# Three stacked graph attention layers: the steps behind a chunk's sums stand earlier and closer together in a table of step numbers

## The chip, the core and the metric

The kernel runs on one core of a Trainium2 chip. A core has five engines with an instruction stream each: TensorE (PE in the profile), VectorE (DVE), ScalarE (ACT), GpSimd (POOL) and SyncE (SP), which here only starts DMAs. An engine takes its instructions strictly in the order in which they are written, and waits at semaphores for the others. The metric is the device time of one execution in microseconds (us), less is better.

## The reference

Three graph attention layers on 3125 nodes, 128 features wide, over the same 103125 edges plus a loop at each node; layers 1 and 2 have a 256-wide hidden part between them, and layers 2 and 3 a layer norm. Each layer is, cut to what matters:

```python
h = x @ W
e = leaky_relu(s[src] + d[dst], 0.2)          # s = h @ a_src, d = h @ a_dst
ex = exp(e - segment_max(e, dst)[dst])
z = segment_sum(ex, dst)
out = segment_sum((ex / z[dst])[:, None] * h[src], dst) + b
```

and the whole: `h = relu(layernorm(x))`, layer 1, `relu`, layer 2, `x = x + ...`, `h = relu(layernorm(x))`, layer 3, `x = x + ...`.

## The kernel before

**Counts instead of edges.** The kernel first (up to about 243 us) turns the edge list into a matrix of counts `C`, 125 partitions wide: how many edges go from each source node to each target. Then every layer is dense: for each target a sum over all sources of count times weight times feature row. Nodes come in 25 tiles of 125.

**Chunks and steps.** The targets are cut into 5 chunks of 5 tiles (625 columns). Three layers of 5 chunks are 15 chunks, `q` = 0 to 14, chunk `q` of layer `q // 5`. A chunk has 25 steps `s`, one for each tile of sources. In a step a block of 125 x 625 weights (`slot[s]`) is made, and PE multiplies it with the feature rows `hB3[:, s]` and adds five sums in PSUM (`products`, L1552; the last two steps L1560). A block is made in one of two ways: by DVE in one instruction (`product`, L924), or by ACT in three (`row_maximum`, L1318, L1321, L1323) and POOL in one (`block_product`, L581). Layer 2 gives the odd steps to ACT and POOL, layer 3 the even ones. ACT works six steps ahead (`PASS_AHEAD`): at its own step s it prepares the block of step s + 6. DVE also computes, for the next chunk's maximum per target, 25 tops (`top_step`, L846 and L848), most of them one to each step.

**What follows a chunk's sums.** Once chunk q - 1 is summed, its result is finished inside the steps of chunk q, by small instructions woven into the streams:

- PE transposes the tops at step `tops` (`top_transpose`, L1522).
- DVE, the chain: `mu` (L858, reads the transposed tops), `e_top` (L861), `m_top` (L864), `back` (L871). Each reads the one before.
- ACT: `kappa` = exp(`back`) (`factors`, L1300). In the stream it stands before the passes of its step.
- DVE, the inverse of the sums: `zk` (L888, needs `kappa`), a reciprocal (L896; in layer 3 L892 and L894), `rz` (L901).
- POOL: `scaled` (L586, needs `rz`) and the addition to `x` (L595). Layer 2: DVE `bn_stats` (L908) and `bn_aggr` (L914), POOL `norm_scalars`, ACT `normalise` (L1264), PE `feat_transposes` (L1575), ACT `copy_featT` (L1235), PE `new_features` (L1608), ACT `new_features` (L1256, L1257).

A table of step numbers sets where each stands. `At(tops, chain, kappa, z, stats, pool, pe, act, rest_pe, rest_act)` has a tuple of steps for each kind of work, and `post_at(q)` picks the row: `USUAL` for most chunks, `BEFORE_LAST` for the last chunk of layers 1 and 2, and `TURN` for a chunk that begins a layer (the turn). A step number is only a place in the streams; nothing but the order depends on it. Chunks 6, 7 and 8 finish chunks of layer 2 by `USUAL[1]`, chunk 9 by `BEFORE_LAST[1]`, chunk 10 by `TURN[1]`, chunks 11 to 14 finish chunks of layer 3 by `USUAL[2]`. Chunk 9 also computes the extremes for layer 3 (L775, L799 at step 6 after an exchange by DMA, and POOL's `scalars` at step 11), and the turn the rest of them (`extremes_late`, L775 again, at step 19), which reads what ACT's `new_features` wrote.

There is a second, slow path (`careful`) for inputs outside a range; these inputs don't take it. It used the table `USUAL` too.

## Time and profile before

| | |
|---|---|
| time, median of 3 runs | 778.18 us (778.1 to 778.4) |
| the profiled execution | 777.95 us, its span 775.9 us, so 2.05 us lie outside the span |
| DVE busy | 713.2 us, 92% of the span |
| PE busy | 664.9 us, 86% |
| ACT busy | 532.1 us, 69% |
| POOL busy | 343.0 us, 44% |
| mean granted TensorE clock | 0.946 |

The span runs from the first to the last instruction that the profiler recorded. Busy time is what an engine spent inside instructions, waits excluded where they come ahead of the instruction. An instruction on DVE is recorded with its own duration, but the next may start before it ends, so the cost of one in a full stream is read from one start to the next.

### The profile page before, as it was taken

The page shows a single profiled execution, that of the slowest core. Times are in us where ns is not written, and L with a number is a line of the kernel's source. Part 1 is how long each engine was busy: PE and PEld are TensorE (multiplying, and loading weights), DVE is VectorE, ACT ScalarE, POOL GpSimd, SP SyncE. Part 2 cuts the span into 40 slices and gives each one's busy share as a digit, 9 for nine tenths or more (in the row PEclk, how much of TensorE's full clock was granted, in tenths as well). Part 3 has the DMA queues.
Part 4 walks back from the last instruction along what each step waited for, and adds up shares of the span by engine and source line. Part 5 has one row for each costly group of instructions (what it writes and reads, how often), then busy time and mean ns, then how long its engine had stood idle before and what let it go on. Part 6 is the DMA issues. An engine that isn't in the chain of part 4 may idle for free.

```text
span 775.9 us, 14060 instructions
## 1 busy us (share of the span) xinstructions
PE 664.9 (86%) x5692; PEld 645.5 (83%) x5692; DVE 713.2 (92%) x935; ACT 532.1 (69%) x814; POOL 343.0 (44%) x305
## 2 busy tenths in 40 slices
PE   4345999898886999999999989999988988998994
PEld 4335888888885989999999989898878888898894
DVE  5499999999976999999999899999999989999994
ACT  0054344444446988778777798898977897898981
POOL 1504000000004555445375556475677666675762
PEclk9997789898876999999999999999999999999997
DMA  3400000000002000000011010000011010100001
GB/s 97 118 0 1 1 1 2 1 1 1 1 1 16 9 17 18 1 17 2 1 8 34 1 25 8 10 17 1 1 8 34 1 25 1 33 23 13 18 1 38
DMA packets 22062, 11.77 MB, mean 15 GB/s; under 512 B 12253, under 2 KB 19915, under 8 KB 21990
## 3 DMA queue, kind: packets, MB, share of 16 engines
q1 hardware_dynamic: 21190, 9.53, 5.5%
q0 software_dynamic: 800, 1.26, 0.6%
q8 instruction: 47, 0.77, 0.5%
q14 instruction: 25, 0.20, 0.1%
HBM read 9.14 MB, written 1.64 MB: 14 GB/s over the span
## 4 chain that ended last, share of the span: by engine, by line
DVE 35%; PE 18%; issue 11%; DMA 2%; POOL 1%; ACT 1%; DVEq 0%; SPq 0%; POOLq 0%
DVE ps L846 18%; PE ps L1552 14%; DVE scratch L924 8%; DVE ps L848 3%; PE ps L1605 1%; DVE mu L858 1%; DMA ext_lines<-ext 1%; PE ps L1583 1%; DMA gathered<-ext_lines 1%; DVE bn6c L908 1%; DVE scratch L846 1%; DVE e_top L861 1%; DVE m_top L864 1%; PE ps L1575 0%; DVE scratch L852 0%
## 5 line engine op out<-in xcount | busy, mean ns | idle before, releaser
L1552 PE MATMUL ps<-hB,scratch 125*125 125x129 f32 x3450 | 408.3, 276 | 34.9 <-DVE scratch L924 27.0
L1552 PEld LDWEIGHTS ps<-hB,scratch 125*125 125x125 f32 x3450 | 392.0, 189 | 47.0 <-DVE scratch L924 38.2
L581 POOL TENSOR_TENSOR scratch<-scratch 125x625 f32<-125x625 f32 x177 | 247.1, 1401 | 181.6 <-ACT scratch L1323 181.4
L846 DVE SCALAR_TENSOR_TENSOR ps<-C,a_unit,ps 125x625 f32<-125x625 uint8 x330 | 279.8, 866 | 2.1
L924 DVE SCALAR_TENSOR_TENSOR scratch<-ps,r_src,C 125x625 f32<-125x625 f32 x198 | 170.7, 862 | 5.4 <-PE ps L1536 5.0
L1487 PE MATMUL ps<-scratch 128*128 128x125 bf16 x1250 | 148.6, 296 | 25.3 <-DVE scratch L760 19.1
L1487 PEld LDWEIGHTS ps<-scratch 128*128 128x128 bf16 x1250 | 143.0, 121 | 29.9 <-DVE scratch L760 23.4
L1323 ACT ACTIVATE scratch<-scratch,r_src 125x625 f32<-125x625 f32 x177 | 158.7, 897 | 0.0
L1318 ACT ACTIVATE scratch<-gathered,r_inv 125x625 f32<-125x625 f32 x177 | 142.9, 807 | 12.8 <-PE ps L1552 10.5
L1198 ACT ACTIVATE C<-ps 125x1750 uint8<-125x1750 f32 (+3 forms) x50 | 74.2, 1488 | 96.9 <-PE ps L1487 96.9
L1321 ACT ACTIVATE scratch<-C 125x625 f32<-125x625 uint8 x177 | 126.3, 714 | 11.1 <-POOL scratch L581 10.8
L760 DVE TENSOR_TENSOR scratch<-key_lo,hB 128x6656 bf16<-128x6656 bf16 (+3 forms) x26 | 94.7, 3642 | 4.5 <-PE ps L1487 4.5
L760 DVE TENSOR_TENSOR scratch<-key_col,hB 128x6500 bf16<-128x6500 bf16 (+3 forms) x26 | 86.0, 3307 | 0.0
L546 POOL TENSOR_TENSOR spread<-extg 125x1 f32<-125x1 f32 x3 | 1.8, 585 | 172.0 <-DVE extg L799 172.0
L1560 PE MATMUL ps<-hB,scratch 125*125 125x129 f32 x300 | 35.5, 273 | 0.0
L1560 PEld LDWEIGHTS ps<-hB,scratch 125*125 125x125 f32 x300 | 34.2, 187 | 0.0
L848 DVE TENSOR_SCALAR ps<-C,a_unit 125x625 f32<-125x625 uint8 x30 | 25.9, 864 | 2.7 <-ACT C L1198 2.6
L1167 ACT ACTIVATE w1T<-ps 128x256 f32<-128x256 f32 x1 | 0.4, 383 | 34.8 <-PE ps L1457 34.8
L1300 ACT ACTIVATE kappa<-back 125x5 f32<-125x5 f32 x15 | 3.1, 208 | 29.4 <-DVE back L871 29.4
L1447 PE MATMUL ps<-ones_b,scratch 125*125 125x1 bf16 x125 | 13.5, 245 | 10.6 <-DVE scratch L705 10.6
L1447 PEld LDWEIGHTS ps<-ones_b,scratch 125*125 125x125 bf16 x125 | 13.4, 230 | 10.6 <-issue 10.6
L586 POOL TENSOR_TENSOR scratch<-scratch,rz 125x640 f32<-125x640 f32 x14 | 17.6, 1258 | 5.9 <-DVE rz L901 5.9
(145 smaller groups left out, 429.9 us busy)
## 6 DMA issues: line engine op xcount, KB each, us to landing
gathered<-g_lines SPq DMA_DIRECT2D x14, 305.2 KB
xr<-in_x SPq DMA_DIRECT2D x1, 1562.5 KB
out<-xr SPq DMA_DIRECT2D x5, 312.5 KB
edge_sb<-in_edges SPq DMA_DIRECT2D x1, 805.7 KB
gathered<-ext_lines SPq DMA_DIRECT2D x5, 122.1 KB
w<-in_W SPq DMA_DIRECT2D x2, 128.0 KB
gathered<-in_edges,start_i POOLq DMA_INDIRECT x5
ext_lines<-ext SPq DMA_DIRECT2D x5, 1.0 KB
```

Of the source, the lines that this page charges most:

```text
L581: g.tensor_tensor(A, A, wide[n % 2], ALU.mult).then_inc(pool_done, 1)
L760: last = v.tensor_tensor(hot[:, g0:g1, :, :], keys.unsqueeze(2).broadcast_to([128, g1 - g0, m, LANES]), iota_t[:, 0:m, :].unsqueeze(1).bro ...
L846: v.scalar_tensor_tensor(dest, counts, unit[:, s:s + 1], top, ALU.min, ALU.max).then_inc(S.top_done, 1)
L848: v.tensor_scalar(dest, counts, unit[:, s:s + 1], None, ALU.min).then_inc(S.top_done, 1)
L924: v.scalar_tensor_tensor(slot[s].rearrange("p (t n) -> p t n", n=P), tiles(ROWU), r_src[L % 2][:, s:s + 1], C5[:, c, s, :].rearrange("p (t ...
L1198: a_.activation(C5[:, c, :, rows].rearrange("p t (w q) -> p t w q", q=WQ), tiles(at_, w1_ - w0).rearrange("p w (t q) -> p t w q", q=WQ), A ...
L1318: a_.activation(A, ga[q % 2], ACT.Relu, bias=-1.0, scale=r_inv[L % 2][:, s:s + 1]).then_inc(over_done, 1)
L1321: a_.activation(wide[k % 2], C5[:, c, s, :], ACT.Copy)
L1323: a_.activation(A, A, ACT.Identity, bias=r_src[L % 2][:, s:s + 1], scale=r_src[L % 2][:, s:s + 1]).then_inc(rowmax_ok, 1)
L1487: last = mm(ps[0:128, o:o + WC], hot_lo[i][:, at_g, :, lane], hot_col[i][:, at_g, :, lane], start=(k == 0), stop=(k == KC - 1))
L1552: last = mm(ps[0:P, acc_at(t):acc_at(t) + HW], A[:, P * t:P * (t + 1)], feat, start=opens and t in (0, 3), stop=closes, skip_group_check=True)
L1560: last = mm(ps[0:P, acc_at(t):acc_at(t) + HW], slot[s][:, P * t:P * (t + 1)], hB3[:, s, :], start=False, stop=s == T - 1, skip_group_check ...
```

## The change

Four rows of the table get other numbers: `USUAL[1]`, `USUAL[2]`, `BEFORE_LAST[1]`, and three numbers in `TURN[1]`. The old `USUAL` is kept under the name `CAREFUL` for the slow path, which so stays as it was. No instruction is added or removed; the first layer's rows are the same. In the diff, with its repeated parts of the slow path cut:

```diff
+        CAREFUL = (At(1, (3, 4, 5, 6), 6, (8, 9, 10), None, (14,), (12, 15, 21), (14, 17, 23), 18, 20),
+                   At(1, (3, 4, 5, 6), 6, (8, 9, 10), (13, 14), (14, 19), (18, None, 21), (16, 20, 23), None, None),
...
         USUAL = (At(1, (3, 4, 5, 6), 6, (8, 9, 10), None, (14,), (12, 15, 21), (14, 17, 23), 18, 20),
-                 At(1, (3, 4, 5, 6), 6, (8, 9, 10), (13, 14), (14, 19), (18, None, 21), (16, 20, 23), None, None),
-                 At(1, (3, 4, 5, 6), 6, (8, 9, 10), None, (14, 17, 20), (None,) * 3, (None,) * 3, None, None))
+                 At(1, (2, 2, 3, 3), 4, (4, 4, 4), (9, 9), (11, 15), (13, None, 15), (13, 14, 17), None, None),
+                 At(1, (2, 2, 3, 3), 4, (4, 4, 4), None, (11, 13, 17), (None,) * 3, (None,) * 3, None, None))
         BEFORE_LAST = (At(1, (3, 4, 5, 6), 6, (8, 9, 10), None, (14,), (12, 14, 19), (13, 16, 21), 17, 18),
-                       At(1, (3, 4, 5, 6), 6, (8, 9, 10), (13, 14), (14, 19), (17, None, 19), (16, 19, 21), None, None))
+                       At(1, (2, 2, 3, 3), 4, (4, 4, 4), (9, 9), (11, 15), (13, None, 15), (13, 14, 17), None, None))
         TURN = (At(None, (1, 1, 2, 2), 3, (3, 3, 3), None, (11,), (7, 9, 13), (9, 12, 15), 11, 13),
-                At(None, (1, 1, 2, 2), 3, (3, 3, 3), (8, 8), (11, 15), (14, None, 16), (13, 14, 17), None, None))
+                At(None, (1, 1, 2, 2), 3, (3, 3, 3), (8, 8), (11, 15), (13, None, 15), (13, 14, 16), None, None))
...
-                at_ = USUAL[q // NC]
+                at_ = CAREFUL[q // NC]
```

DVE in chunk 8 (layer 2), from step 3 to step 6, before. L924 is a block, L846 a top, the rest are the small steps; a row's bracket names the semaphores that it waits for:

```order
L846 SCALAR_TENSOR_TENSOR ps<-C,a_unit,ps 125x625 [waits top_done] x2
L858 TENSOR_REDUCE mu<-ps 125x5 [waits top_T]
L924 SCALAR_TENSOR_TENSOR scratch<-ps,r_src,C 125x625 [waits rows_ready,pe_done]
L846 SCALAR_TENSOR_TENSOR ps<-C,a_unit,ps 125x625 [waits top_done]
L861 SCALAR_TENSOR_TENSOR e_top<-mu,b_low 125x5 [waits top_max,back_low]
L846 SCALAR_TENSOR_TENSOR ps<-C,a_unit,ps 125x625 [waits top_done]
L864 SCALAR_TENSOR_TENSOR m_top<-e_top 125x5 [waits m_lin]
L924 SCALAR_TENSOR_TENSOR scratch<-ps,r_src,C 125x625 [waits rows_ready,pe_done]
L846 SCALAR_TENSOR_TENSOR ps<-C,a_unit,ps 125x625 [waits top_done]
L871 SCALAR_TENSOR_TENSOR back<-m_top,back_of 125x5 [waits kappa_ready,m_lin]
```

The same place in the changed kernel, steps 2 to 4, whose lines are numbered 3 higher:

```order
L849 SCALAR_TENSOR_TENSOR ps<-C,a_unit,ps 125x625 [waits top_done]
L861 TENSOR_REDUCE mu<-ps 125x5 [waits top_T]
L864 SCALAR_TENSOR_TENSOR e_top<-mu,b_low 125x5 [waits top_max,back_low]
L849 SCALAR_TENSOR_TENSOR ps<-C,a_unit,ps 125x625 [waits top_done]
L867 SCALAR_TENSOR_TENSOR m_top<-e_top 125x5 [waits m_lin]
L874 SCALAR_TENSOR_TENSOR back<-m_top,back_of 125x5 [waits kappa_ready,m_lin]
L927 SCALAR_TENSOR_TENSOR scratch<-ps,r_src,C 125x625 [waits rows_ready,pe_done]
L849 SCALAR_TENSOR_TENSOR ps<-C,a_unit,ps 125x625 [waits top_done]
L891 TENSOR_TENSOR zk<-scratch,kappa 125x5 [waits raw_ready,kappa_ready]
L899 RECIPROCAL zk<-zk 125x5 [waits z_lin]
L904 TENSOR_TENSOR rz<-zk,kappa 125x5 [waits raw_used,z_lin]
```

Before, every small instruction had a block or a top between itself and the one that it reads; now four pairs (five with `bn_stats` and `bn_aggr`) are direct neighbours, and `mu` comes one top earlier.

DVE in chunk 12 (layer 3) in the changed kernel, steps 1 to 4:

```order
L927 SCALAR_TENSOR_TENSOR scratch<-ps,r_src,C 125x625 [waits rows_ready,pe_done]
L849 SCALAR_TENSOR_TENSOR ps<-C,a_unit,ps 125x625 [waits top_done] x2
L861 TENSOR_REDUCE mu<-ps 125x5 [waits top_T]
L864 SCALAR_TENSOR_TENSOR e_top<-mu,b_low 125x5 [waits top_max,back_low]
L927 SCALAR_TENSOR_TENSOR scratch<-ps,r_src,C 125x625 [waits rows_ready,pe_done]
```

Before, the second L927 here and one more top stood ahead of `mu`: it comes two instructions earlier.

PE in the turn of layer 3 (chunk 10), where L1575 and L1608 are the transposes and the new features, before and then in the changed kernel:

```order
L1552 MATMUL ps<-hB,scratch 125x129 x75
L1575 MATMUL ps<-ident,scratch 128x125 x5
L1552 MATMUL ps<-hB,scratch 125x129 x10
L1608 MATMUL ps<-w,scratch 125x130 x5
L1552 MATMUL ps<-hB,scratch 125x129 x30
```

```order
L1555 MATMUL ps<-hB,scratch 125x129 x70
L1578 MATMUL ps<-ident,scratch 128x125 x5
L1555 MATMUL ps<-hB,scratch 125x129 x10
L1611 MATMUL ps<-w,scratch 125x130 x5
L1555 MATMUL ps<-hB,scratch 125x129 x35
```

Both moved one step (five matmuls) ahead.

## Rows read from the trace of the kernel before

**Rows 1.** The page, busy time and share of the span of each engine.
```profile
PE 664.9 (86%) x5692; PEld 645.5 (83%) x5692; DVE 713.2 (92%) x935; ACT 532.1 (69%) x814; POOL 343.0 (44%) x305
```

**Rows 2.** Busy time by stretch: chunk 8; order PE, PEld, DVE, ACT, POOL, clock, DMA.
```profile
525.50:559.00 33.50, 31.32 (x275) 30.55 (x275) 33.32 (x57) 29.93 (x50) 21.15 (x18) 1.00 0.01 1
```

**Rows 3.** Timeline, DVE in chunk 8: start, duration, what (x2: two of them).
```profile
528.65 1.64 DVE L846 SCALAR_TENSOR_TENSOR ps<-C,a_unit,ps 125x625 f32<-125x625 uint8 x2
...
544.54 0.84 DVE L846 SCALAR_TENSOR_TENSOR ps<-C,a_unit,ps 125x625 f32<-125x625 uint8 x1
```

**Rows 4.** Timeline, DVE in chunk 10, the turn, steps 1 to 9.
```profile
598.52 0.80 DVE L858 TENSOR_REDUCE mu<-ps 125x5 f32<-125x625 f32 x1
599.44 0.17 DVE L861 SCALAR_TENSOR_TENSOR e_top<-mu,b_low 125x5 f32<-125x5 f32 x1
599.54 0.87 DVE L924 SCALAR_TENSOR_TENSOR scratch<-ps,r_src,C 125x625 f32<-125x625 f32 x1
...
601.10 0.16 DVE L864 SCALAR_TENSOR_TENSOR m_top<-e_top 125x5 f32<-125x5 f32 x1
...
601.38 0.87 DVE L846 SCALAR_TENSOR_TENSOR ps<-C,a_unit,ps 125x625 f32<-125x625 uint8 x1
602.15 0.16 DVE L888 TENSOR_TENSOR zk<-scratch,kappa 125x5 f32<-125x5 f32 x1
...
602.73 0.87 DVE L924 SCALAR_TENSOR_TENSOR scratch<-ps,r_src,C 125x625 f32<-125x625 f32 x1
...
608.23 1.06 DVE L908 BATCH_NORM_STATS2 bn6c<-xr 125x6 f32<-125x128 f32 x5
...
609.68 0.84 DVE L846 SCALAR_TENSOR_TENSOR ps<-C,a_unit,ps 125x625 f32<-125x625 uint8 x1
```

**Rows 5.** Timeline, PE and DVE behind the last chunk; brackets: idle before, releaser.
```profile
764.78 0.71 PE L1522 MATMUL ps<-ident,scratch 125*125 125x125 f32 x5
765.52 0.81 DVE L858 TENSOR_REDUCE mu<-ps 125x5 f32<-125x625 f32 x1 [3.33 <-PE ps L1522]
...
767.28 0.17 DVE L888 TENSOR_TENSOR zk<-scratch,kappa 125x5 f32<-125x5 f32 x1 [0.27 <-ACT kappa L1300]
...
767.91 0.17 DVE L901 TENSOR_TENSOR rz<-zk,kappa 125x5 f32<-125x5 f32 x1
```

**Rows 6.** Timeline, PE and POOL at the head of chunk 8.
```profile
528.77 0.71 PE L1522 MATMUL ps<-ident,scratch 125*125 125x125 f32 x5
...
531.28 1.52 POOL L581 TENSOR_TENSOR scratch<-scratch 125x625 f32<-125x625 f32 x1 [1.70 <-ACT scratch L1323]
```

**Rows 7.** Timeline, heads of chunk 12 and, the last row, of chunk 13.
```profile
672.01 0.71 PE L1522 MATMUL ps<-ident,scratch 125*125 125x125 f32 x5
672.21 0.87 DVE L924 SCALAR_TENSOR_TENSOR scratch<-ps,r_src,C 125x625 f32<-125x625 f32 x1
...
676.16 1.29 POOL L581 TENSOR_TENSOR scratch<-scratch 125x625 f32<-125x625 f32 x1 [1.19 <-ACT scratch L1323]
676.88 0.60 DVE L864 SCALAR_TENSOR_TENSOR m_top<-e_top 125x5 f32<-125x5 f32 x1
...
683.04 0.86 DVE L924 SCALAR_TENSOR_TENSOR scratch<-ps,r_src,C 125x625 f32<-125x625 f32 x1
...
705.12 1.51 POOL L581 TENSOR_TENSOR scratch<-scratch 125x625 f32<-125x625 f32 x1 [0.61 <-ACT scratch L1323]
```

**Rows 8.** Timeline, PE and DVE in the turn, chunk 10, steps 14 to 19.
```profile
617.74 2.37 PE L1552 MATMUL ps<-hB,scratch 125*125 125x129 f32 x20
...
622.18 0.17 DVE L775 TENSOR_SCALAR a_neg<-ab 125x10 f32<-125x10 f32 x1 [3.14 <-ACT ab L1257]
```

**Rows 9.** Timeline, DVE in chunk 9.
```profile
573.62 1.07 DVE L901 TENSOR_TENSOR rz<-zk,kappa 125x5 f32<-125x5 f32 x1
...
578.79 1.07 DVE L908 BATCH_NORM_STATS2 bn6c<-xr 125x6 f32<-125x128 f32 x5 [0.91 <-POOL xr L595]
```

**Rows 10.** Timeline, DVE in chunk 11.
```profile
641.97 1.31 DVE L861 SCALAR_TENSOR_TENSOR e_top<-mu,b_low 125x5 f32<-125x5 f32 x1
```

More of the change, by code:

```diff
@@ L346, in gat_stack_kernel @@
         At = namedtuple("At", "tops chain kappa z stats pool pe act rest_pe rest_act")
+        CAREFUL = (At(1, (3, 4, 5, 6), 6, (8, 9, 10), None, (14,), (12, 15, 21), (14, 17, 23), 18, 20),
+                   At(1, (3, 4, 5, 6), 6, (8, 9, 10), (13, 14), (14, 19), (18, None, 21), (16, 20, 23), None, None),
+                   At(1, (3, 4, 5, 6), 6, (8, 9, 10), None, (14, 17, 20), (None,) * 3, (None,) * 3, None, None))
         USUAL = (At(1, (3, 4, 5, 6), 6, (8, 9, 10), None, (14,), (12, 15, 21), (14, 17, 23), 18, 20),
-                 At(1, (3, 4, 5, 6), 6, (8, 9, 10), (13, 14), (14, 19), (18, None, 21), (16, 20, 23), None, None),
-                 At(1, (3, 4, 5, 6), 6, (8, 9, 10), None, (14, 17, 20), (None,) * 3, (None,) * 3, None, None))
+                 At(1, (2, 2, 3, 3), 4, (4, 4, 4), (9, 9), (11, 15), (13, None, 15), (13, 14, 17), None, None),
+                 At(1, (2, 2, 3, 3), 4, (4, 4, 4), None, (11, 13, 17), (None,) * 3, (None,) * 3, None, None))
         BEFORE_LAST = (At(1, (3, 4, 5, 6), 6, (8, 9, 10), None, (14,), (12, 14, 19), (13, 16, 21), 17, 18),
-                       At(1, (3, 4, 5, 6), 6, (8, 9, 10), (13, 14), (14, 19), (17, None, 19), (16, 19, 21), None, None))
+                       At(1, (2, 2, 3, 3), 4, (4, 4, 4), (9, 9), (11, 15), (13, None, 15), (13, 14, 17), None, None))
         TURN = (At(None, (1, 1, 2, 2), 3, (3, 3, 3), None, (11,), (7, 9, 13), (9, 12, 15), 11, 13),
-                At(None, (1, 1, 2, 2), 3, (3, 3, 3), (8, 8), (11, 15), (14, None, 16), (13, 14, 17), None, None))
+                At(None, (1, 1, 2, 2), 3, (3, 3, 3), (8, 8), (11, 15), (13, None, 15), (13, 14, 16), None, None))
         EXPS = {(0, 0): 1, (1, 0): 2, (1, EARLY_TILES): 3, (1, LATE): 4, (2, 0): 5, (2, EARLY_TILES): 6, (2, LATE): 7}
@@ L1408, in careful_chunk @@
                             careful_sums(q - 1)
-                        after_sums(K, q - 1, USUAL[L], s)
+                        after_sums(K, q - 1, CAREFUL[L], s)
                     if s == LEAD - 1:
@@ L1431, in careful @@
                     for s in range(T):
-                        after_sums(K, L * NC + NC - 1, USUAL[L], s)
+                        after_sums(K, L * NC + NC - 1, CAREFUL[L], s)
             act.wait_ge(mode_ready, 1)
@@ L1716, in careful_chunk @@
                     if c:
-                        after_sums(K, q - 1, USUAL[L], s)
+                        after_sums(K, q - 1, CAREFUL[L], s)
             def careful():
@@ L1727, in careful @@
                     for s in range(T):
-                        after_sums(K, L * NC + NC - 1, USUAL[L], s)
+                        after_sums(K, L * NC + NC - 1, CAREFUL[L], s)
             pe.wait_ge(mode_ready, 1)
```

## The prediction

> **What bounds the kernel now.** I read the page first: DVE is the busiest engine, 713.2 us of the span [rows 1]. Then the busy time by stretch, one stretch to a chunk: in chunk 8 DVE is busy 33.32 of 33.50 us, PE 31.32, ACT 29.93, POOL 21.15 [rows 2], and the other inner chunks of layers 2 and 3 look alike. DVE's stream there has no holes; a chunk lasts as long as DVE's instructions do, laid one behind the other. So a move of steps can gain only where DVE stands still or is held up inside an instruction, and everything that it adds to DVE's stream is paid. That PE, ACT or POOL get a result sooner is worth nothing unless DVE waits for it.
>
> Then the timeline of DVE for its costs from one start to the next. A block or a top costs 0.775 us wherever it stands: from the first top of the pair at 528.65 to the top at 544.54 lie 15.89 us [rows 3] with 17 of them (11 tops, 6 blocks), 13.17 us, so the small steps of a whole chunk of layer 2 cost only 2.72 us: `mu` about 0.72, `bn_stats` and `bn_aggr` 1.32, and the other six 0.07 to 0.11 each, for they overlap with the large neighbour, plus 0.24 held up. In layer 3, chunk 12, from 672.21 to 683.04 are 10.83 us [rows 7] with 11 large ones, 8.53: 2.30 for the small ones.
>
> Last, the holds. Some small DVE instructions last far longer than their 0.15: `m_top` at 676.88 lasts 0.60 and ends at 677.48, and POOL's instruction from 676.16 ends at 677.45 [rows 7]. `e_top` in chunk 11 lasts 1.31 [rows 10], `rz` in chunk 9 1.07 [rows 9], each until a POOL instruction ends. Over the trace this holds for `e_top`, `m_top`, `back`, `zk`, `rz` and L892 whenever they start inside a POOL tensor instruction, and never for `mu`, the reciprocals, blocks and tops. The section "Who interferes with whom" of the Trainium skill's page "SBUF — State Buffer" states that a VectorE instruction with two SBUF inputs and a GpSimd instruction that reads SBUF exclude each other, the later one waiting to the end of the earlier; the trace agrees, for example in the 0.60.
>
> **The change, part by part.**
>
> *Neighbours that depend on each other.* The turns already have the close pattern, so its price can be read in chunk 10 [rows 4]: `mu` to the block behind `e_top` 1.02 (0.92 of it before `e_top` starts), `m_top` to the top behind `back` 0.28, `zk` to the block behind `rz` 0.58, `bn_stats` to the top behind `bn_aggr` 1.45. Sum 3.33 us, without holds. Apart, the same steps cost 2.72 - 0.24 = 2.48. So +0.85 in each of the chunks 6 to 9. In layer 3 there are no statistics and one pair more: `zk` to `rz` over L892 and L894 is 767.28 to 767.91, 0.63 [rows 5], and about 0.09 more, in all 1.02 + 0.28 + 0.72 = 2.02.
>
> The section "The DRAIN you can't avoid" of the Trainium skill's page "VectorE: DVE Perf Modes" states that a semaphore between chained VectorE instructions costs nothing extra. By it this whole term would be zero; the pairs in chunk 10 disagree, and I go by them.
>
> *`mu` waits for PE's transposes.* They keep their place. In chunk 8 they run to 528.77 + 0.71 = 529.48 [rows 6]; a waiting `mu` starts 0.03 behind their end (764.78 + 0.71 = 765.49, start 765.52 [rows 5]), so at 529.51. DVE is there at 528.65 + 0.775 = 529.42 [rows 3]: a wait of 0.09. In chunk 12 they end at 672.72, and `mu` could start where the block at 672.21 stood [rows 7]: a wait of 0.54. These transposes follow the product of step 1, which follows DVE's own block of step 1, so the wait can't shrink; chunks 13 and 14 give the same. In chunk 11 PE ran later and I read 0.8.
>
> *Holds, layer 2.* In chunks 7 and 8 `m_top` will start at 529.51 + 0.92 + 0.10 + 0.775 = 531.31, and POOL's block of step 9 starts at 531.28 [rows 6], in chunk 7 at the same distance. That is a tie within what the rows resolve. If DVE comes second it stands until 532.80, 1.35 us more than the 0.19; if POOL does, nothing. The bounds are 0 and 1.35 per chunk. No row shows two that close; I take half, 0.7, for each of the two. All later small steps fall where POOL waits for ACT's next pass, and the 0.24 of before goes. So chunks 7 and 8: 3.33 + 0.09 - 2.72 = +0.70 each, and 0.7 each for the tie; chunk 6 +0.7 with a little hold on either side of the change. In chunk 9 three tiny instructions stand at step 1, so that `m_top` comes at 565.05, 0.2 behind POOL's start: held 1.3. Against that the hold of `rz` (0.9), the wait of `bn_stats` for POOL (0.91) [rows 9] and a 0.35 wait for the exchange by DMA go, since `rz` comes ahead of POOL's `scalars`: 4.82 after against 5.07 before, -0.25.
>
> What is late next in chunk 9: DVE reaches L799 nearly 2 us later, behind 1.3 of hold and the three inverse steps; POOL's `scalars` (3.6 us) and its blocks of steps 11 and 13 wait for it, and PE comes to the transposes before `normalise` is done, about 2 us idle. PE would then be through to the rows of the next chunk at about 594.9, and DVE wants them at 595.2. That cover is only 0.3 us; a further us lost there would be paid in full.
>
> *Holds, layer 3.* `kappa` is now released at step 3 instead of 6, ACT saves its wait of 2 to 4 us per chunk and comes early into the next, as it does today into chunk 13. There POOL starts the block of step 8 at 705.12 and is busy until 706.63 [rows 7], and `e_top` would start at about 706.03: held 0.6. I take 0.55 for chunks 12, 13 and 14 (bounds 0 and 1.3). Behind it POOL idles until `kappa`. So chunk 12: 2.02 + 0.54 + 0.55 - 2.30 = +0.81; chunks 13 and 14 in the same way +0.36 and +0.81; chunk 11, where the hold of `e_top`, 1.2, and one of L892 go: -0.53. Sum +1.45.
>
> *The turn, chunk 10.* DVE stands 3.14 us at step 19 for `new_features` [rows 8]. PE's transposes and matmuls stand one step earlier now. A step of PE is 1.10 us (617.74 to 619.94 are two, with PE never idle [rows 8]). `normalise` ends 1.0 before the earlier place, and the copy of the features 1.1 before the earlier matmuls, so neither stops it, and ACT has no pass between steps 16 and 17. Gain 1.10; the rest of the 3.14 stays. Everything behind (POOL's scalings, the exponentials, the exchange) moves with it.
>
> *What costs nothing.* POOL's and ACT's other steps move past blocks of their own queue, whose readers are steps away; the cover is that PE takes a block five steps or more after POOL made it. `normalise` in chunks 7 and 8 ends about 1.3 us before PE asks for it. No DMA is moved on SP's queue.
>
> **Sum.** Chunks 6, 7, 8: +2.1; chunk 9: -0.25; chunk 10: -1.1; chunks 11 to 14: +1.45. Together +2.2, and +1.35 for the tie (0 to +2.7): +3.5. Against the profiled execution's 777.95, which lies 0.23 below the median, this is 781.5 us.
>
> **The rivals.**
>
> *The later starts miss POOL everywhere.* POOL is busy 21.15 of 33.50 us in a chunk [rows 2], and my phases rest on differences of 0.1 to 0.5 us. Without the tie, the 1.3 of chunk 9 and the three 0.55 the sum is 2.2 - 1.3 - 1.65 = -0.8: 777.2 us, not slower. It decides once the new holds fall below about 2 us in all. For it: DVE is the later one only by little. Against it: in layer 3 the overlap is half an instruction deep.
>
> *Dependent neighbours cost nothing in a full stream.* Then 0.85 x 4 and in layer 3 0.78 x 4 (2.02 against 1.24) go, 6.5 us: 777.95 + 3.5 - 6.5 = 775.0, faster. Only the page's rule speaks for it, and the turn's rows are from a stream just as full.
>
> *Chunk 9 becomes the bound.* If POOL's late blocks let PE reach the turn's rows 2 us or more after DVE, the cover of 0.3 is gone and chunk 9 adds 2 to 4: 784 to 785. For it: PE already waits there today.
>
> *The move does nothing*, since DVE's stream has the same instructions: 778.2. That would need costs and gains to cancel.
>
> **Chances.** The forecast (dearer neighbours, new holds, tie either way) 0.68, its own range 779.6 to 783.5. No holds 0.13; neighbours free 0.05; chunk 9 the bound 0.07; cancelling 0.07. The measurement tells about 0.2%, 1.6 us, from no change. Slower 0.73, within 0.16, faster 0.11. Range with the other cases 777.0 to 784.3.
>
> **What the changed profile would show.** In chunk 8, `mu` directly followed by `e_top` 0.92 later, `back` 0.19 behind `m_top`, the stretch from the top of step 2 to that of step 15 about 16.6 (18 with the tie lost) instead of 15.89; `m_top` either 0.15 or 1.5 long; in chunks 12 to 14 an idle of 0.5 before `mu`, and `e_top` about 0.7 long; L775 in the turn with an idle of 2.0 instead of 3.14; ACT's wait at `kappa` near zero or below 1 us. What would make me wrong: `m_top` and `e_top` short everywhere, an idle before L775 that shrinks by more than a step, or a new idle of DVE at the head of chunk 10.

## The result and the profile after

The changed kernel takes 784.35 us, median of 6 runs (782.75 to 786.67); the kernel before, in runs on the same chip, 778.16 (777.46 to 779.12, 6 runs). The ratio is 1.0078, with a 95% interval of 1.0062 to 1.0094: slower by 6.2 us. The time is above the forecast's own range (779.6 to 783.5) and 0.05 above the end of the range with the other cases, 784.3. The profiled execution took 786.67 us, its span 784.6.

The busy times move little against [rows 1] (DVE by 3.2 us, with its holds in them) while the span grew by 8.7; where the loss is can't be seen in them:

```profile
PE 666.5 (85%) x5692; PEld 649.6 (83%) x5692; DVE 716.4 (91%) x935; ACT 534.0 (68%) x814; POOL 343.1 (44%) x305
```

So the chunks have to be measured one by one. Each chunk ends its tops with one join (L852; L855 in the changed kernel, whose lines all stand 3 higher); I took the start of each join from the timelines, and the table gives the time from one to the next, called the chunk's period below. The last column is from the last join to DVE's first write-out behind `rz`. Two traces each of the kernel before and of the changed one (the second is an experiment below):

| us in chunk | 1 to 5 | 6 | 7 | 8 | 9 | 10 | 11 | 12 | 13 | 14 | end |
|---|---|---|---|---|---|---|---|---|---|---|---|
| before | 177.28 | 35.16 | 33.55 | 33.53 | 36.34 | 38.87 | 35.48 | 32.35 | 32.82 | 32.36 | 6.72 |
| before, second trace | 177.36 | 35.16 | 33.53 | 33.53 | 36.50 | 38.87 | 35.49 | 32.36 | 32.81 | 32.35 | 6.71 |
| changed | 177.30 | 35.58 | 35.39 | 35.41 | 35.97 | 37.77 | 37.18 | 33.15 | 33.37 | 33.15 | 7.11 |
| changed, second trace | 177.26 | 35.58 | 35.40 | 35.40 | 35.98 | 37.75 | 36.80 | 33.15 | 33.37 | 33.15 | 7.11 |

The part ahead of the first join, which no edit touches, took 273.4 to 276.5 us in the 13 traces of this case. It is most of the scatter of the times, and 1.7 of the 8.7 us by which the changed kernel's first trace is longer. From chunk 6 on the periods of one kernel repeat to a few hundredths, but for two: chunk 9 with its old row took 36.25 to 36.73 in six traces, as its wait for the exchange by DMA was 0.24 to 0.75 long, and chunk 11 differs by 0.38 between the changed kernel's traces. So the periods, not the totals, decide what follows. Behind the first join the changed kernel's first trace is 7.0 us longer than the first of before, and the second 6.2 us longer than the second.

**Chunks 7 and 8: +1.85 each.** Timeline of chunk 7 in the changed kernel, all engines:

```profile
499.86 1.54 POOL L584 TENSOR_TENSOR scratch<-scratch 125x625 f32<-125x625 f32 x1 [1.80 <-ACT scratch L1326]
499.88 0.16 DVE L867 SCALAR_TENSOR_TENSOR m_top<-e_top 125x5 f32<-125x5 f32 x1
500.07 1.35 DVE L874 SCALAR_TENSOR_TENSOR back<-m_top,back_of 125x5 f32<-125x5 f32 x1
501.35 0.86 DVE L927 SCALAR_TENSOR_TENSOR scratch<-ps,r_src,C 125x625 f32<-125x625 f32 x1
```

The tie was there to within 0.02 us. `m_top` slipped past POOL, and the next one, `back`, lay 0.19 behind it and was held to 501.42, 0.02 after POOL's end. It is no chance: in both chunks of all four traces with this row POOL starts 0.01 to 0.02 ahead of `m_top`, and `back` is 1.35 long. (The kernels further below with the same row are layer 2 alone and the last one.)

**Chunk 11: +1.70, where I had -0.53.** PE around the head of chunk 11 (its timeline), then DVE and ACT (timeline of all engines), then the same time in stretches of 2 us; behind the five busy times stand the granted clock, DMA's share and GB/s:

```profile
635.12 2.37 PE L1563 MATMUL ps<-hB,scratch 125*125 125x129 f32 x20
639.57 4.09 PE L1555 MATMUL ps<-hB,scratch 125*125 125x129 f32 x20 [2.09 <-ACT scratch L1295]
643.50 0.71 PE L1525 MATMUL ps<-ident,scratch 125*125 125x125 f32 x5
```

```profile
644.25 0.81 DVE L861 TENSOR_REDUCE mu<-ps 125x5 f32<-125x625 f32 x1 [2.38 <-PE ps L1525]
645.17 0.76 DVE L864 SCALAR_TENSOR_TENSOR e_top<-mu,b_low 125x5 f32<-125x5 f32 x1
...
649.18 0.21 ACT L1303 ACTIVATE kappa<-back 125x5 f32<-125x5 f32 x1 [4.85 <-DVE back L874]
```

```profile
638.00:640.00 2.00, 0.43 (x2) 0.46 (x3) 2.00 (x3) 2.00 (x5) 1.39 (x2) 0.89 0.29 12
640.00:642.00 2.00, 2.00 (x11) 2.00 (x11) 1.87 (x3) 1.82 (x3) 0.75 (x2) 0.50 0.43 64
642.00:644.00 2.00, 2.00 (x16) 2.00 (x15) 0.00 (x0) 1.91 (x3) 1.41 (x1) 0.76 0.28 1
```

PE stood idle 2.09 us for ACT, and as it went on its granted clock was 0.50, that is 1.2 instead of 2.4 GHz: 20 products (two steps of a chunk, since the profile counts ten to a step) took 4.09 us, not 2.37 to 2.47. `mu` waits behind them for the transposes, and DVE is busy 0.00 from 642 to 644.

**Chunks 12 to 14** show what I had forecast; chunk 12 in the timeline, a wait of `mu` of 0.44, then `e_top` held to the end of POOL's block, 0.73 long:

```profile
678.08 0.71 PE L1525 MATMUL ps<-ident,scratch 125*125 125x125 f32 x5
...
678.83 0.81 DVE L861 TENSOR_REDUCE mu<-ps 125x5 f32<-125x625 f32 x1 [0.44 <-PE ps L1525]
679.17 1.29 POOL L584 TENSOR_TENSOR scratch<-scratch 125x625 f32<-125x625 f32 x1 [0.83 <-ACT scratch L1326]
679.75 0.73 DVE L864 SCALAR_TENSOR_TENSOR e_top<-mu,b_low 125x5 f32<-125x5 f32 x1
```

**The turn** gives 1.10: DVE's wait at the row of [rows 8] is now

```profile
626.57 0.17 DVE L778 TENSOR_SCALAR a_neg<-ab 125x10 f32<-125x10 f32 x1 [1.91 <-ACT ab L1260]
```

**The end** is 0.39 longer; against the 3.33 of [rows 5] DVE's timeline shows

```profile
774.15 0.81 DVE L861 TENSOR_REDUCE mu<-ps 125x5 f32<-125x625 f32 x1 [3.72 <-PE ps L1525]
```

### The profile page after: what moved, and what is told of

It is laid out like the page before. It is cut to its first block, busy times and chain, and to the rows that moved or that the text cites. A ratio compares the mean times of both kernels' runs of the same rounds, so it can differ in the third digit from the quotient of the medians.

```text
span 784.6 us, 14060 instructions
## 1 busy us (share of the span) xinstructions
PE 666.5 (85%) x5692; PEld 649.6 (83%) x5692; DVE 716.4 (91%) x935; ACT 534.0 (68%) x814; POOL 343.1 (44%) x305
## 4 chain that ended last, share of the span: by engine, by line
DVE 34%; PE 22%; issue 10%; ACT 2%; DVEq 0%
PE ps L1555 18%; DVE ps L849 17%; DVE scratch L927 9%; DVE ps L851 3%; DVE mu L861 2%; PE ps L1608 1%; PE ps L1586 1%; DVE scratch L849 1%; ACT scratch L1326 1%; DVE bn6c L911 0%; ACT scratch L1321 0%; DVE m_top L867 0%; PE ps L1578 0%; DVE scratch L855 0%; PE ps L1525 0%
## 5 line engine op out<-in xcount | busy, mean ns | idle before, releaser
L927 DVE SCALAR_TENSOR_TENSOR scratch<-ps,r_src,C 125x625 f32<-125x625 f32 x198 | 170.2, 860 | 5.4 <-PE ps L1539 5.0
L1303 ACT ACTIVATE kappa<-back 125x5 f32<-125x5 f32 x15 | 3.1, 207 | 32.6 <-DVE back L874 32.6
```

Source lines behind the costliest of these rows:

```text
L927: v.scalar_tensor_tensor(slot[s].rearrange("p (t n) -> p t n", n=P), tiles(ROWU), r_src[L % 2][:, s:s + 1], C5[:, c, s, :].rearrange("p (t ...
```

## The experiments

Each kernel is a whole computation; only rows of the table differ. Periods are compared with the table above, first traces. The low clock stretches stand at different places from execution to execution, and the part ahead of the first join scatters, so the times say less than the periods.

### The turn alone

Against the kernel before, only:

```diff
-                At(None, (1, 1, 2, 2), 3, (3, 3, 3), (8, 8), (11, 15), (14, None, 16), (13, 14, 17), None, None))
+                At(None, (1, 1, 2, 2), 3, (3, 3, 3), (8, 8), (11, 15), (13, None, 15), (13, 14, 16), None, None))
```

> The changed kernel with the old rows for the inner chunks of layers 2 and 3 and for chunk 9; only the three numbers of the turn stay changed. Theory (the turn gives back exactly one step of TensorE, whatever the neighbouring chunks do): chunk 10 takes 37.77 us as in the changed kernel, against 38.87 before; the wait ahead of a_neg in the turn 2.0 instead of 3.14; all other chunks within 0.2 of before; time about 777.1 us against 778.2. Rival (the turn's gain depends on chunk 9's new row, since the turn begins where chunk 9 ends): chunk 10 gains under 0.5. The trace tells it; the time alone, a gain of 0.14%, hardly can. The clock is a side question: where before and the changed kernel differ in the place of TensorE's low-clock stretch around chunks 10 and 11, this kernel with old rows in chunk 11 should keep it in chunk 10 (granted clock under 1 between 626 and 632) or at least outside chunk 11's head.

Measured: 778.14 us (10 runs) against 779.13 (19 runs), ratio 0.9986 (0.9976 to 0.9996). Chunk 10 took 37.64, the wait ahead of `a_neg` 1.92; chunks 6, 7, 8, 11 to 14 are within 0.1 of before, chunk 9 is +0.24 with its DMA wait at 0.57 instead of 0.35. The turn's gain, 1.1 to 1.2 us, is its own. The side guess on the clock failed: the low stretch stood at the head of chunk 11 here too (0.66 and 0.50 from 636 to 640), with chunk 11 at 35.38, since the old row has `mu` 0.6 us behind the transposes' end.

### Layer 2 alone

`USUAL[1]` and `BEFORE_LAST[1]` new, the other rows old.

> Only the rows of layer 2 (chunks 6, 7, 8 and chunk 9) are new. Theory (dearer neighbours, and a hold of 1.35 on back in chunks 7 and 8 where POOL's block of step 9 starts just ahead): periods against before +0.4 in chunk 6, +1.8 each in chunks 7 and 8, -0.4 in chunk 9, nothing elsewhere: +3.7, 781.9 us. Rival (the tie with POOL falls either way from execution to execution): one or both of chunks 7 and 8 come out at +0.5, and the time at 779.2 to 780.6. Second rival (the steps behind slip too, so that chunk 9's late POOL work shows in chunk 10): chunk 10 above 38.87 by 0.3 or more.

Measured: 784.65 us (4 runs), ratio 1.0059 (1.0042 to 1.0076), that is +4.6; the medians are 5.5 apart, as the periods of this trace are. Chunks 6 to 9: 35.58, 35.39, 35.39, 35.97, to 0.02 the changed kernel's. But chunk 10 took 40.65 instead of 38.87: the second rival. Up to step 13 of chunk 10 the streams of this kernel and of the changed one are the same, so the two can be laid side by side. PE in the changed kernel, its own timeline, then in this one:

```profile
588.42 0.75 PE L1578 MATMUL ps<-ident,scratch 125*128 125x125 f32 x5 [1.87 <-ACT scratch L1267]
589.01 2.37 PE L1555 MATMUL ps<-hB,scratch 125*125 125x129 f32 x20
...
600.04 0.71 PE L1539 MATMUL ps<-ident,g_row 125*125 125x125 f32 x5
```

```profile
589.50 0.75 PE L1578 MATMUL ps<-ident,scratch 125*128 125x125 f32 x5 [1.86 <-ACT scratch L1267]
590.10 4.03 PE L1555 MATMUL ps<-hB,scratch 125*125 125x129 f32 x20
...
602.78 0.71 PE L1539 MATMUL ps<-ident,g_row 125*125 125x125 f32 x5
```

and DVE here, whose same block followed without a wait in the changed kernel:

```profile
603.63 0.87 DVE L927 SCALAR_TENSOR_TENSOR scratch<-ps,r_src,C 125x625 f32<-125x625 f32 x1 [1.54 <-PE ps L1539]
```

From the first product of the twenty to the rows of the next chunk are 11.03 us there and 12.68 here. Here PE's granted clock was 0.57 and 0.58 from 590 to 594, there 1.00 in the stretches from 588 to 594. This is the cover of 0.3 us that I had named for chunk 9: measured 0.16 (rows done 5.75 behind the join, DVE's block at 5.91; before, the rows were done at 5.46). The new row thinned the cover from 0.45 to this, and a low clock behind PE's last wait is then paid by DVE. With the old row it isn't: in layer 3 alone the clock was low from 582 to 585, but this lay ahead of the place where PE waits 1.72 us for ACT's `normalise` in the trace of before, and took that wait's place. PE there, without an idle ahead of L1578:

```profile
580.95 6.33 PE L1555 MATMUL ps<-hB,scratch 125*125 125x129 f32 x40 [1.91 <-DVE scratch L927]
587.33 0.75 PE L1578 MATMUL ps<-ident,scratch 125*128 125x125 f32 x5
```

The forty products took 6.33 instead of 4.67 us, and chunk 10 its usual 38.86. The kernels with the old places and with `mu` back at step 3 show the same (38.87).

### Layer 3 alone

`USUAL[2]` new, the other rows old.

> Only the row of layer 3 (chunks 11 to 14) is new. In the changed kernel chunk 11 took 1.70 us more than before where I had forecast 0.53 less; mu waited 2.38 there for TensorE. Theory A (the granted clock fell at the head of chunk 11 in the changed kernel, 0.50 from 640 to 642, because the turn and chunk 9 before it ran otherwise; the table of chunk 11 itself costs what I forecast): with the old rows ahead the clock falls in chunk 10 as before, mu waits about 0.8, chunk 11 comes out at -0.5, and the sum is -0.5 +0.8 +0.55 +0.8 and 0.4 at the end: +2.0, 780.2 us. Theory B (the row of chunk 11 makes DVE come so early that it waits about 2.4 for TensorE at any clock): chunk 11 at +1.7 with granted clock 1 around its head, +4.2 in all, 782.4 us. Chunks 12, 13, 14 at +0.8, +0.55, +0.8 in either, with mu waiting 0.45 in each.

Measured: 782.95 us (4 runs), ratio 1.0051 (1.0034 to 1.0069), +4.0 (medians 3.8 apart). Chunks 11 to 14: 36.78, 33.37, 33.36, 33.16, the end 7.09; +1.30, +1.02, +0.54, +0.80, +0.37, together 4.0. In chunk 11 `mu` waited 2.38 again, so theory A's sum fell. But neither is theory B as written shown, for the clock was not 1: it was 0.59 and 0.55 from 636 to 640. With old rows ahead the clock can fall at the head of chunk 11 all the same; whether the wait needs that fall was left to the next runs. The difference of 0.4 to the changed kernel's first trace in chunk 11 is `e_top`, 0.76 long there and 0.38 here; in chunk 12 `e_top` is 0.92 long here and 0.73 there.

### Old places, but the inverse and the statistics close

Against the kernel before, in `USUAL[1]` and `BEFORE_LAST[1]`; in `USUAL[2]` the first edit alone:

```diff
-(8, 9, 10), (13, 14)
+(8, 8, 8), (13, 13)
```

> Everything as before the change but for the closeness: zk, the reciprocals and rz stand at one step (8, 8, 8 instead of 8, 9, 10), and bn_stats and bn_aggr at one step (13, 13 instead of 13, 14), in the inner chunks of layers 2 and 3 and in chunk 9. Nothing comes sooner, the turn is the old one. Theory (a dependent direct neighbour costs 0.12 to 0.2 us more than one with a block between): zk to the block behind rz 0.58 instead of three times 0.09, bn_stats to the top behind bn_aggr 1.45 instead of 1.32: chunks 6, 7 and 8 at +0.45 each (33.55 to about 34.0), layer 3 +0.3 to +0.4 each less the hold of L892 where there was one (0.4 to 0.7 in chunks 11 to 14), so about -0.2 each: in all +0.5, 778.7 us. Rival (neighbours cost nothing, all of the loss of the changed kernel was holds and waits): chunks 6, 7, 8 within 0.1 of 33.5, and the time about 776.5 from the holds that go.

Measured: 780.05 us (10 runs), ratio 1.0007 (0.9997 to 1.0016). Chunks 6, 7, 8 and 9: 35.65, 34.01, 34.02, 36.80, so +0.49, +0.46, +0.49, +0.46, where the theory said 0.45 and the rival 0. Layer 3: 34.95, 32.15, 32.35, 32.15, that is -0.53, -0.20, -0.47, -0.21, the holds of L892 that go. DVE's timeline in chunk 7 shows the price as the turn did in [rows 4]: from `zk` to the top behind `rz` 0.56, and 1.46 around the statistics.

```profile
505.27 0.15 DVE L891 TENSOR_TENSOR zk<-scratch,kappa 125x5 f32<-125x5 f32 x1
505.53 0.19 DVE L899 RECIPROCAL zk<-zk 125x5 f32<-125x5 f32 x1
505.75 0.17 DVE L904 TENSOR_TENSOR rz<-zk,kappa 125x5 f32<-125x5 f32 x1
505.83 0.87 DVE L849 SCALAR_TENSOR_TENSOR ps<-C,a_unit,ps 125x625 f32<-125x625 uint8 x1
...
511.26 1.06 DVE L911 BATCH_NORM_STATS2 bn6c<-xr 125x6 f32<-125x128 f32 x5
512.36 0.45 DVE L917 BATCH_NORM_AGGREGATE mvc<-bn6c 125x2 f32<-125x6 f32 x5
512.72 0.84 DVE L927 SCALAR_TENSOR_TENSOR scratch<-ps,r_src,C 125x625 f32<-125x625 f32 x1
```

### Layer 2, with `m_top` and `back` past POOL's block

Against layer 2 alone, in its two new rows:

```diff
-(2, 2, 3, 3), 4, (4, 4, 4)
+(2, 2, 4, 4), 4, (5, 5, 5)
```

> Layer 2's rows as in the changed kernel, but m_top and back one step later (chain 2, 2, 4, 4) and the inverse too (5, 5, 5); layer 3 and the turn old. Theory (the loss of 1.84 and 1.88 in chunks 7 and 8 is 1.35 of hold behind POOL's block of step 9 plus 0.5 for the dependent neighbours): m_top comes about 1.55 later, when POOL's block is over, back lasts 0.2 instead of 1.35, chunks 7 and 8 +0.4 to +0.6 against before, chunk 6 +0.4, chunk 9 -1.2 to -1.6 (its hold goes too); in all 0 against before. Rival (the close chain itself costs it, not POOL): chunks 7 and 8 stay at +1.8 with short small steps. Second question, the cover of PE at the end of chunk 9: if TensorE's clock falls in chunk 9's last steps, DVE waits for L1539 in chunk 10 as in the run with layer 2 alone (1.54 there); with chunk 9 shorter PE's slack is larger or equal, so chunk 10 should be 38.9 unless it falls there.

Measured: 780.13 us (10 runs), ratio 1.0020 (1.0010 to 1.0030). Chunks 6 to 9: 35.42, 34.23, 34.22, 35.15: +0.26, +0.68, +0.69, -1.19. The hold is gone (timeline of chunk 7, all engines):

```profile
497.74 1.51 POOL L584 TENSOR_TENSOR scratch<-scratch 125x625 f32<-125x625 f32 x1 [1.81 <-ACT scratch L1326]
...
499.31 0.16 DVE L867 SCALAR_TENSOR_TENSOR m_top<-e_top 125x5 f32<-125x5 f32 x1
499.50 0.17 DVE L874 SCALAR_TENSOR_TENSOR back<-m_top,back_of 125x5 f32<-125x5 f32 x1
```

What is left, 0.68, is the 0.70 of the forecast without the tie; in chunk 6 the kernel before had `m_top` 0.84 long, a hold of 0.69 and not of 0.24, and 0.70 + 0.24 - 0.69 is the +0.26. On the second question the case that I had named came: the clock was low from 583 to 587, right behind a wait of PE of 2.53, and chunk 10 took 40.98, DVE waiting 1.86 for PE's rows. The periods add up to +2.6 and the medians are 1.4 apart, so whether every timed execution paid this is open.

### Layer 3, with `mu` back at step 3

Only `USUAL[2]` differs from the kernel before:

```diff
-                 At(1, (3, 4, 5, 6), 6, (8, 9, 10), None, (14, 17, 20), (None,) * 3, (None,) * 3, None, None))
+                 At(1, (3, 3, 4, 4), 4, (5, 5, 5), None, (11, 13, 17), (None,) * 3, (None,) * 3, None, None))
```

> Only layer 3's row is new, with mu back at step 3 and the rest behind it (chain 3, 3, 4, 4; kappa 4; inverse 5, 5, 5). Theory (in layer 3 the loss is mu's wait for TensorE, 2.38 in chunk 11 and 0.45 in the others, and the hold of e_top): with mu one step later DVE never waits there, even where TensorE's clock falls to 0.50 at the head of chunk 11 as it did in the run with layer 3 alone; chunk 11 about 34.5 (34.95 with the old chain and the inverse together), chunks 12, 13, 14 about 32.1, 32.1, 32.1 (32.35, 32.80, 32.35 before): in all -1.8 against before, 777.3 us. Rival (the closeness is what costs, 2.02 against 1.24 for the small steps): chunks 12 to 14 at +0.3 to +0.8 against before with no idle ahead of mu.

Measured: 777.38 us (10 runs), ratio 0.9982 (0.9970 to 0.9994): faster. Chunks 11 to 14: 34.11, 32.05, 32.05, 32.07, so -1.37, -0.30, -0.77, -0.29; the end 7.10, +0.38. No DVE wait in chunks 11 to 14, though the clock was 0.62 and 0.53 at the head of chunk 11. The periods add up to -2.4, the medians are 1.3 apart; in this trace the part up to chunk 5 is 0.9 longer than in that of before. The steps are as close here as in the changed kernel, and the chunks are shorter than before: the holds of `m_top` and L892 that go (0.60 long in [rows 7]) outweigh the dearer neighbours. So what cost in layer 3 was `mu` one step too soon, together with the hold of `e_top` that it brings, and not the closeness.

### The kernel before once more

No edit.

> The kernel before once more, for a second trace of the same streams. In its first trace the granted clock of TensorE was 0.50 at the end of chunk 10 (627.6 to 631.6); in the five traces of other kernels since then it was 0.50 at the head of chunk 11, right behind an idle of 2.08 of TensorE. Theory (the place of the low stretch varies from execution to execution, more than with the table): the low stretches of layers 2 and 3 stand elsewhere than in the first trace, and the periods of chunks 6 to 14 are the same as before within 0.1 but for chunk 9 (its wait for the exchange by DMA varied between 0.35 and 0.75), since with the old tables DVE has cover from TensorE there. Rival (the table sets the place): the low stretch is again from 627 to 632 counted from the same join.

Measured: 779.94 us, one run. The rival held for the clock: the low stretch stood at the end of chunk 10 again, 0.50 from 630 to 632, at the same distance from the join as in the first trace. The periods are the same. PE's timeline:

```profile
629.49 4.13 PE L1552 MATMUL ps<-hB,scratch 125*125 125x129 f32 x20 [1.17 <-POOL scratch L581]
...
637.04 2.44 PE L1552 MATMUL ps<-hB,scratch 125*125 125x129 f32 x20 [0.67 <-ACT scratch L1292]
639.32 0.71 PE L1522 MATMUL ps<-ident,scratch 125*125 125x125 f32 x5
```

The slow twenty come ahead of PE's wait for ACT here and are absorbed in it: the wait is 0.67 instead of 2.08. That is why the trace of before showed PE ready for `mu` early. Both traces of the kernel before have the low stretch here, and all ten others that have one near the turn have it at the head of chunk 11, those with old rows around it too; whether the table or chance moves it is open.

### The changed kernel once more

No edit.

> The changed kernel once more, for a second trace of the same streams. Theory (the new rows leave DVE with no cover from TensorE in two places, so that a low stretch of the clock that falls there is paid in full): chunks 6, 7, 8 at 35.6, 35.4, 35.4 as in the first trace; chunk 10 either 37.8, or 39.3 with an idle of 1.5 ahead of DVE's first block if the clock falls in the last steps of chunk 9 (as in the run with layer 2 alone); chunk 11 37.2 with mu waiting 2.4 if it falls at that chunk's head, 35.5 with mu waiting 0.8 if it doesn't. Rival (the waits belong to the table): both traces alike, mu waits 2.4 whatever the clock.

Measured: 786.42 us, one run. Chunks as in the table; `mu` waited 2.38 in chunk 11 with low clock there again (0.54 and 0.60). One low stretch of the first trace, from 574 to 578, is missing and another, in chunk 7, came again; chunk 10 took 37.75, without the wait.

### The parts that gained, together

The turn's new row, layer 3 as above, layer 2 and chunk 9 as before the change.

> The parts that gained by themselves, put together: layer 2 and chunk 9 with the old rows, the turn's new row, layer 3 with mu at step 3 and the rest close behind it (3, 3, 4, 4; 4; 5, 5, 5). Theory (the parts add up): -1.2 in the turn, -1.4, -0.3, -0.75, -0.3 in chunks 11 to 14, +0.4 at the end, against the timed kernel before -3.5: 775.2 us where before stands at 778.7. Rival (what DVE gains in one chunk is given back where TensorE is then late): the gain stays under 2 us, with new idles of DVE in chunk 11 or at the end.

Measured: 774.48 us (773.20 to 775.70, 5 runs) against 778.29 (9 runs), ratio 0.9954 (0.9940 to 0.9968): 3.8 us faster than the kernel before by the medians, 3.6 by the ratio. Chunks 9 to 14: 36.25, 37.65, 34.11, 32.03, 32.06, 32.06, the end 7.11. The parts add up (-3.7 in the periods). This execution had no low clock in layers 2 and 3 up to the last join, and so tells what chunk 11 left open. Its PE timeline:

```profile
633.58 2.44 PE L1555 MATMUL ps<-hB,scratch 125*125 125x129 f32 x20 [2.08 <-ACT scratch L1295]
635.86 0.71 PE L1525 MATMUL ps<-ident,scratch 125*125 125x125 f32 x5
```

The wait for ACT is the same 2.08, but the twenty products take 2.44, and the transposes end 9.78 us behind the join. In all four traces with the new row of layer 3 they ended 11.43 or 11.44 behind it. 1.65 of `mu`'s 2.38 is thus the clock; the other 0.73 is the table's, near the 0.8 that I had read. This is inferred across kernels, since no trace of the changed kernel itself is without that low stretch. With `mu` at step 3 the clock costs nothing: chunk 11 takes 34.11 here without the low stretch and 34.11 with it in the kernel that has layer 3's row alone.

### The mix, with the sooner row in chunk 9

Against the mix, in `BEFORE_LAST[1]`:

```diff
-                        At(1, (3, 4, 5, 6), 6, (8, 9, 10), (13, 14), (14, 19), (17, None, 19), (16, 19, 21), None, None))
+                        At(1, (2, 2, 4, 4), 4, (5, 5, 5), (9, 9), (11, 15), (15, None, 17), (13, 16, 19), None, None))
```

> As the mix of the parts that gained, and chunk 9 with the sooner row whose m_top and back stand at step 4, but with TensorE's transposes and new features two steps later (15 and 17 instead of 13 and 15; ACT's copy and the new features 16 and 19). Theory (DVE's wait of 1.5 to 1.9 ahead of its first block in chunk 10, seen in two kernels with the new chunk 9, comes from TensorE's idle of 1.9 to 2.5 for normalise, plus the low clock behind it; two steps later the transposes never wait): TensorE's idle ahead of the transposes under 0.3, its rows for the next chunk done 4.5 to 5.5 us behind the join instead of 5.7 to 7.7, no wait of DVE there at any clock, chunk 9 at 35.1 and chunk 10 at 37.7: 1.2 us faster than the mix without it, 774.0. Rival (the low clock alone makes TensorE late): chunk 10 at 39.3 or more with the idle gone.

Measured: 775.29 us (5 runs), ratio 0.9957 (0.9943 to 0.9971): no gain over the mix. Chunk 9 took 35.16 as hoped, chunk 10 39.70. PE's timeline, then DVE's row in chunk 10:

```profile
587.41 1.37 PE L1611 MATMUL ps<-w,scratch 128*125 128x130 f32 x10 [1.85 <-ACT scratch L1238]
588.62 7.34 PE L1555 MATMUL ps<-hB,scratch 125*125 125x129 f32 x50
```

```profile
596.64 0.87 DVE L927 SCALAR_TENSOR_TENSOR scratch<-ps,r_src,C 125x625 f32<-125x625 f32 x1 [1.82 <-PE ps L1539]
```

The idle ahead of the transposes is gone, but PE now waits 1.85 ahead of the new features, for ACT's copy at step 16, and the clock is low behind that. Chunk 10 is as long as the rival said, but the idle is not gone: my change of the two steps only moved it.

### The changed kernel, with PE's feature steps later

`BEFORE_LAST[1]` with the same (15, None, 17), (13, 16, 19); otherwise the changed kernel.

> The changed kernel, only with TensorE's transposes and new features of chunk 9 two steps later (15 and 17 instead of 13 and 15; ACT's copy and new features 16 and 19). In the changed kernel TensorE stood 1.87 us there for normalise and was through with the rows for chunk 10 5.75 us behind the join, where DVE wanted them at 5.91. Theory: the idle goes, the rows are done 4.5 to 5.5 behind the join, DVE never waits for them; since the changed kernel's two traces don't show the wait either, the periods stay (36.0 in chunk 9, 37.8 in chunk 10) and the time is the changed kernel's, 784.3, or up to 0.7 below it if some of its executions pay the wait. Chunks 6, 7, 8 again +0.4, +1.85, +1.85, chunk 11 with mu waiting 2.4 behind the low clock. Rival (TensorE's lateness is set by POOL's late blocks of steps 11 and 13, not by normalise): the idle moves to a block of POOL and the rows are done no earlier than 5.7.

Measured: 785.79 us (4 runs), ratio 1.0090 (1.0069 to 1.0111), not to be told from the changed kernel. PE waited 1.51 for ACT's copy; the rows for chunk 10 were done 5.63 behind the join, and DVE didn't wait for them, with no low clock there. Neither theory holds: the cover grew by 0.1 only. Placing ACT's copy sooner was not tried.

## Why the prediction was right or wrong

The direction was right, the time 2.85 us short. The largest miss, 2.2 of the 3.5 us by which the first trace's periods exceed the forecast's sum, is chunk 11; the tie gives 0.9 and the end 0.4. The direction was no luck: without chunk 11's miss the change would still have lost over 4 us in that trace. By its own steps, with the measured periods (the changed kernel's two traces, the first against the first of before, the second, where it differs, against the second):

| chunk | forecast | measured |
|---|---|---|
| 6 | +0.7 | +0.42 |
| 7 and 8, each | +0.7 and the tie 0 to 1.35 (0.7 taken) | +1.84 to +1.88 |
| 9 | -0.25 | -0.37, -0.52 |
| 10 | -1.10 | -1.10 |
| 11 | -0.53 | +1.70, +1.31 |
| 12, 13, 14 | +0.81, +0.36, +0.81 | +0.80, +0.55, +0.79 |
| end | 0 | +0.39 |

*Dear neighbours*: right, and shown apart from all else by the kernel with the old places (+0.46 to +0.49 for its part) and by layer 2 without the hold (+0.68 for 0.70). In chunk 6 the hold of before was larger than I had allowed. The section "The DRAIN you can't avoid" of the Trainium skill's page "VectorE: DVE Perf Modes" says of a chain of copies that a semaphore behind each of them costs nothing extra. I had drawn from it the rival that dependent neighbours are free, and this fell. The rule itself is not tested here, since no run has the same neighbours without their semaphores. One reading of mine was too wide: a top does not cost 0.775 "wherever it stands", for at the head of chunk 10 five in a row start 0.90 to 0.91 apart (591.02, 591.92, 592.83); no term of the sum used it there.

*The tie*: the mechanism was right, and the term, "half, 0.7", mis-sized: it cost 1.15 in both chunks of both traces, always the same way (35.39 with the hold, 34.23 without). I had asked only whether `m_top` comes before POOL. Two small steps stand there 0.19 apart. POOL's recorded start lies 0.01 to 0.02 ahead of the first, which was not held all the same (the rows don't resolve why), and the second pays. A pair of dependent neighbours is a wider target than one instruction.

*`mu` waits for PE*: 0.44 for the 0.54 forecast in chunks 12 to 14. In chunk 11 the step that failed is "in chunk 11 PE ran later and I read 0.8". I took PE's times from one trace in which the low clock had fallen just ahead of a wait that absorbed it, and put no term for its falling elsewhere. In 10 of the 13 traces it fell behind that wait; then the transposes end 1.42 to 1.67 later. The old row has `mu` at 11.9 to 12.3 behind the join and is covered at either place (chunk 11 took 35.38 or 35.39 in three traces with the old row and the low clock at its head); the new row wants it at 9.1. That is 1.65 of the 2.23 and 1.84 missed there in the two traces. The rest goes to the hold of `e_top`, 0.76 and 0.38 long in chunk 11, where I had none. (My list of the steps that POOL holds names `zk` too; no `zk` of the trace of before starts inside a POOL instruction, so that one isn't shown.)

*The end*: not in my sum, without a reason given. In the changed kernel PE runs 180 products of the last chunk (18 steps) without a gap:

```profile
751.15 20.21 PE L1555 MATMUL ps<-hB,scratch 125*125 125x129 f32 x180 [0.85 <-DVE scratch L927]
```

It lost time at the head of the chunk, waiting for DVE's blocks, and doesn't catch up. The same +0.4 stands in every kernel with a new row of layer 3, also where DVE's chunk got shorter; what sets it is argued, not tested.

*Chunk 9 becomes the bound*: this rival did not show in the changed kernel's two traces, but it did in layer 2 alone (+1.78), with `m_top` later (+2.11) and in the mix with chunk 9 (+2.05 against the mix). It did not come as I had put it, with PE 2 us late by POOL's blocks: the new row thins the cover from 0.45 to 0.16, and the wait comes when a low stretch falls behind PE's last idle ahead of the rows, as it did in these three traces and not in the changed kernel's two. How many of the changed kernel's timed executions paid it is open.

*ACT's wait at `kappa` near zero*: wrong. It was 4.85 in chunk 11 and 32.6 us in all, against 29.4 before. The rows of the costliest groups, of the page of before and then of the changed kernel (busy time, mean, idle before it, and what ended it):

```profile
L1300 ACT ACTIVATE kappa<-back 125x5 f32<-125x5 f32 x15 | 3.1, 208 | 29.4 <-DVE back L871 29.4
L1303 ACT ACTIVATE kappa<-back 125x5 f32<-125x5 f32 x15 | 3.1, 207 | 32.6 <-DVE back L874 32.6
```

A step number asks for `kappa` sooner, and ACT then stands sooner too; its wait moves, it isn't saved. The holds of `e_top` in chunks 12 to 14 rested on this saving: they came out near the forecast (0.73, 0.94 and 0.73 long, so 0.56, 0.77 and 0.56 of hold for 0.55), since POOL's block started 9.2 us behind the join where I had taken 8.9 from chunk 13, but the reason that I gave for its place is not what the trace shows, and that part of the agreement is luck.

## What to carry to other kernels

Moving a small dependent step sooner costs where its neighbour, its producer or another engine's lock now stands: price the step by the start-to-start distances of a place that already has the pattern, and look for a lock in the whole width of the pair. Before slack is spent, subtract the longest delay that the late engine can show, here 1.65 us from one low stretch of PE's clock, and ask what it would do on either side of the next wait. A second trace of the same kernel costs little, but it is no proof: that of the kernel before had the low stretch at the same harmless place as the first, and only other tables' traces showed it elsewhere. Then test the parts apart: the change lost 6.2 us as a whole, while the turn's part and a layer 3 one step later gained 3.8 together.

## What the runs showed of the hardware

**A low stretch and its price.** TensorE's clock fell to a granted 0.50 (1.2 GHz) for 3.4 us at a time: 0.89, 0.50 and 0.76 over 2 us each at the head of chunk 11 make 3.4 us at half speed. Twenty products that lay in it took 4.03 to 4.13 us instead of 2.37 to 2.47, so one stretch costs some 1.65 us.

**What PE did before.** The 13 traces have 25 low stretches in layers 2 and 3 up to the last join. Each begins at most 0.5 us ahead of, or 1.5 us behind, PE's first product after an idle: 1.17 us long in the two traces of the kernel before, 1.85 to 2.86 in all others. But not each such idle has one. Identical streams had them at different places: the changed kernel from 503.0 and from 574.7, its second trace only from 503.6 in that layer. At the head of chunk 11 eleven traces have an idle of 2.08 or 2.09 us and ten of them a low stretch behind it; the mix has none. What decides between the idles is open.

**Holds of VectorE by GpSimd.** `e_top`, `m_top`, `back`, `rz` and L892, which are 0.15 to 0.17 us long alone, lasted up to 1.36 us when they started inside a POOL instruction on a block, until 0.02 to 0.03 us behind its end. Where `m_top` started 0.01 to 0.02 us behind POOL's start, in both chunks of four traces, it was not held, and `back`, 0.19 later, was.
